# Cross-attention and quantized feed-forward on one core: the values are weighed between the two pairs of scores

## What is computed

```python
h = layernorm(x)
q = h @ Wq
k, v = split(concat(ctx, h) @ Wkv)          # 77 + 1024 keys, 16 heads of 16
dots = q @ k.T * 16 ** -0.5                  # per head
dots = where(j > i + 77, -inf, dots)         # a query sees the context and the rows up to its own
x = x + softmax(dots) @ v @ Wout + bout
h = layernorm(x)
x = x + quant_linear(gelu(quant_linear(h, w_fc)), w_proj)   # 256 -> 1024 -> 256
```

## Time and profile before

| | |
|---|---|
| median of 3 runs | 704.45 us |
| lowest and highest | 699.52 and 713.93 us |
| the profiled execution | 706.0 us |
| its span | 704.3 us |
| mean granted PE clock | 0.908 |
| PE busy | 605.6 us (86%) |
| VectorE busy | 424.8 us (60%) |
| ScalarE busy | 422.4 us (60%) |
| GpSimd busy | 217.7 us (31%) |

### The profile page before, as it was taken

The page is one execution under the profiler, slowest core; times in us unless marked ns, Lnnn a source line. Parts: engine busy times, 40 slices in busy tenths (PEclk is TensorE's granted clock), DMA queues, the critical chain, the costliest instruction groups (busy, mean ns, idle before and its releaser), DMA issues.

```text
span 704.3 us, 11805 instructions
## 1 busy us (share of the span) xinstructions
PE 605.6 (86%) x4138; PEld 265.5 (38%) x4147; DVE 424.8 (60%) x925; ACT 422.4 (60%) x555; POOL 217.7 (31%) x312
## 2 busy tenths in 40 slices
PE   8478887999998897997988899999998997978833
PEld 4323443334453342333543144334542463335411
DVE  5504869668755685498364468484277295374554
ACT  3165565688646964875565576876676565645701
POOL 3225601441526221441344212441435212121100
PEclk9879898999999998999998699999997797689975
DMA  4998921340499623092696203093896021003102
GB/s 142 123 168 141 106 80 41 75 53 16 71 112 130 92 61 105 1 120 55 87 120 99 39 16 88 4 112 62 106 136 84 16 61 46 16 16 62 31 15 46
DMA packets 77703, 52.04 MB, mean 74 GB/s; under 512 B 37771, under 2 KB 77319, under 8 KB 77626
## 3 DMA queue, kind: packets, MB, share of 16 engines
q1 hardware_dynamic: 77626, 51.02, 47.2%
HBM read 12.12 MB, written 4.19 MB: 23 GB/s over the span
## 4 chain that ended last, share of the span: by engine, by line
PE 52%; DVE 26%; issue 8%; DMA 6%; ACT 5%; SPq 2%; POOL 1%; DVEq 0%; ACTq 0%
PE psO L1222 15%; PE psS L1237 12%; PE psD L1157 6%; PE psD L1103 5%; DVE hid L870 4%; PE psD L1137 4%; PE psD L1155 3%; ACT probs L720 3%; DMA k_stack<-k_parts 3%; DVE amax L859 3%; PE psD L1166 3%; PE psD L1113 3%; DMA hT<-hq 2%; DVE hq L871 2%; DVE o_cols L990 2%
## 5 line engine op out<-in xcount | busy, mean ns | idle before, releaser
L720 ACT ACTIVATE probs<-psS 128x1024 f32<-128x1024 f32 (+4 forms) x392 | 329.5, 887 | 202.6 <-PE psS L1237 201.6
L663 POOL TENSOR_SCALAR_AFFINE_SELECT probs<-probs 128x512 f32<-128x512 f32 (+2 forms) x164 | 105.7, 656 | 375.9 <-ACT probs L720 375.9
L1237 PE MATMUL psS<-q_stack,k_stack 99*128 99x512 bf16 (+5 forms) x1008 | 201.8, 316 | 18.7 <-ACT probs L720 9.8
L1222 PE MATMUL psO<-probs,v_aug 128*17 128x512 f32 (+5 forms) x2016 | 184.5, 473 | 20.6 <-DVE o_cols L990 17.0
L1237 PEld LDWEIGHTS psS<-q_stack,k_stack 99*128 99x128 bf16 (+1 forms) x1008 | 81.2, 104 | 149.4 <-ACT probs L720 76.7
L1222 PEld LDWEIGHTS psO<-probs,v_aug 128*17 128x17 f32 (+1 forms) x2016 | 44.7, 99 | 110.0 <-issue 96.2
L859 DVE TENSOR_REDUCE amax<-hid 128x32 f32<-128x1024 f32 (+1 forms) x45 | 53.4, 1187 | 28.5 <-ACT hid L793 27.1
L990 DVE STREAM_TRANSPOSE o_cols<-psO 128x512 f32<-128x512 f32 (+1 forms) x36 | 23.5, 653 | 70.3 <-PE psO L1222 70.0
L870 DVE TENSOR_TENSOR hid<-hid,magic 128x1024 f32<-128x1024 f32 (+1 forms) x45 | 56.7, 1261 | 11.0 <-DMA hT<-hq 5.4
L793 ACT ACTIVATE hid<-psD 128x512 f32<-128x512 f32 x64 | 37.4, 597 | 43.0 <-PE psD L1157 42.6
L871 DVE TENSOR_TENSOR hq<-hid,magic 128x1024 bf16<-128x1024 f32 (+1 forms) x41 | 53.2, 1298 | 1.4
(11 more groups left out here) (90 smaller groups left out, 531.3 us busy)
## 6 DMA issues: line engine op xcount, KB each, us to landing
q_stack<-q_parts SPq DMA_DIRECT2D x96, 128.0 KB, 5.2
k_stack<-k_parts SPq DMA_DIRECT2D x48, 147.2 KB, 8.1
k_stack<-k_parts SPq DMA_DIRECT2D x48, 128.0 KB, 6.0
x_in<-in_x_dram SPq DMA_DIRECT2D x8, 512.0 KB, 4.6
x<-in_x_dram SPq DMA_DIRECT2D x8, 512.0 KB, 4.7
out_dram<-x SPq DMA_DIRECT2D x16, 256.0 KB, 2.2
hid<-in_L_ffn_w_fc_dram SPq DMA_DIRECT2D x1, 1024.0 KB, 17.1
hid<-in_L_ffn_w_proj_dram SPq DMA_DIRECT2D x1, 1024.0 KB, 5.0
```

What stands on the lines that cost most here:

```text
L663: last = pool.affine_select(out=tile, in_=tile, compare_op=ALU.is_ge, fill=0.0, base=first - (P * t - CTX), pattern=[[0, GH], [1, m]], cha ...
L720: act.activation(probs[:, k % PB, 2 * pair:2 * pair + 2, 0:n], psS[:, 2 * pair:2 * pair + 2, 0:n], ACT.Exp, scale=DH ** -0.5).then_inc(pro ...
L1222: last = pe.matmul(psO[SQ * j:SQ * j + VW, first - st.q0:first - st.q0 + n], v_aug[0:rows, v_tile(st.b, st.c, t), GH * st.g + j, :], probs ...
L1237: last = pe.matmul(psS[0:rows, j, off:off + n], k_stack[0:ROWS, GH * st.g + j, P * t:P * t + rows], q_heads(0, ROWS, st)[:, j, first - CHU ...
```

## The change

In each turn PE weighs the values after the first half's items and ahead of the second pair of scores, where it weighed them behind that pair. Nothing else is edited; the places in the table stay.

```diff
                 if 0 <= k < TOTAL:
                     for item in PLAN[k, 0]:
                         handle(item)
-                if k + 1 < TOTAL:
-                    score_pair(k + 1, 1)
                 if 1 <= k:
                     for n in PV_AT[k]:
                         pv(n)
+                if k + 1 < TOTAL:
+                    score_pair(k + 1, 1)
                 for item in PLAN[k, 1]:
                     handle(item)
```

## The result

The change makes the kernel slower: 726.23 us (median of 5 runs, 716.03 to 727.25) against 710.63 (5 runs), a ratio of 1.033 with a 95% interval of 1.020 to 1.045. Timed again beside other kernels it was 715.28 us (4 runs) against 708.59, 1.016 (1.004 to 1.028). The ratios leave out runs in a second, slower state that some executions fall into, so they are not the quotients of the medians, which are 1.022 and 1.009. The forecast was 708 us, within 697 to 719, and +3.7 us; the medians are +15.6 and +6.7 us apart.

What follows compares the result with a forecast made beforehand. PE, busy 86% of the span, was taken as the bound. Terms 3.4 + 1.7 + 2.4 + 2 - 1.8 - 2 - 2 = +3.7 us, on a median of 704.45, gave 708 us, range 697 to 719.

Steps and rivals of the forecast that it cites:

- Worth at most those 9.8 us: PE's waits for exponentials: giving PE work between two pairs of scores could by itself gain at most 9.8 us.
- the copy places: 15 places where ScalarE's copy falls behind the second exponential: PE waits 6.8 us in all, half taken, 3.4 us lost.
- Turns without items: 85 of 195 turns: the new order is the same cycle turned by one place, so the cost is nothing.
- The credit for score waits: Scores where two weighings now come ahead of the second pair: early waits go, -2 us, between 0 and -9.8.
- fc behind a second pair: Five fc runs: a later exponential delays the first gelu, so the fourth fc waits 0.35 us each, 1.7 us lost.
- The wait for psO and the masks: Second pair now behind four psO waits, 2.4 us lost; weighings come earlier behind later masks, 2 us lost.
- What comes earlier: A block's last weighing ends 0.44 us sooner: wout's waits for attT give -1.8 us, xqT's input -2.0 us.
- The signs: If right: score waits 13 to 20 us, on first pairs; attT below 7.5; psO near 17; ScalarE's score waits about 200.
- the slower rival: ScalarE's queue can't follow back-to-back exponentials in turns with items, PE waits: 721 us, +16.5 us; chance 0.13.
- The faster rival: VectorE's chain starts 0.44 us sooner at 14 places and weighings cover score waits: 693 us, 11 us gained; chance 0.14.
- Rival C: Posed with the experiments: whole kernel's time follows the granted clock, which got lower; no chance given.

Runs made afterwards that it cites:

- experiments 1: Against the kernel before, the weighing moved ahead of the second pair only in the 83 turns with first-half items: 723.17 us, 1.020.
- 7: Kernel before, with every exponential over half of its columns only: 710.37 us, 1.003 of the untouched kernel before.
- 8: Full change, with every exponential over half of its columns only: 702.29 us, 0.999 of the untouched kernel before.
- 9: Kernel before, but turns weighing two steps without first-half items put both weighings ahead of the second pair: 712.54 us, 1.012.
- 10: Kernel before, but turns weighing two steps put one weighing ahead of the second pair, the other behind: 711.74 us, no ratio.
- 11: Kernel before, with ScalarE's copies of first-half items ahead of its second exponential: 708.08 us, 1.003.
- number 2: Against the kernel before, the weighing moved ahead of the second pair only in the 112 turns without first-half items: 712.71 us, 1.006.
- 3: Full change, with ScalarE's copies of first-half items ahead of its second exponential: 717.46 us, 1.011 of before.
- 4: Full change, with all items of a turn in its second half: 712.46 us, 1.005 of before.
- 6: Full change, but the weighing stays behind the second pair in the 36 turns after a block's opening step: 716.74 us, 1.018 of before.

## Why the prediction was wrong

*The bound and the views.* Right: PE is the engine that sets the time, and its busy time didn't change. "Worth at most those 9.8 us" was right for a gain; it said nothing on how fast the same number can grow, and I took a small number of waits for room.

*Turns with items: the copy places.* The mechanism and the places were right, and the term was mis-sized in one move. Worked out were 6.8 us at 15 places; measured are 7.1 - 0.7 = 6.4 us. "I take half the sum, 3.4, as PE waits for VectorE or attT between most of them" is what failed: at most 2 of the 6.4 us can have been given back, as PE's waits for attT, xqT's input and psO fell by 5.8 us together, where 3.8 were forecast for other reasons. At the weighing of psO, the largest such wait, 16.3 us of 17.0 remain. That VectorE is fed by PE, so that the wait behind such a place starts later with it, would explain this; no run tests it. The Trainium skill (PSUM — Partial Sum Buffer, Engine vs sequencer instructions) says that ScalarE's queue is strictly first in, first out. The trace agrees with that order (cast at 133.88, exponential behind it at 134.34), and the undiscounted 6.8 us was the better guide.

*Turns without items.* "As a cycle these are the same string" is the step that failed outright. It holds only while each turn weighs once. The second turn of each block weighs nothing, and there the weighing of the turn before used to part the pairs. The third steps of the blocks carry about 18 us of excess instead of 7.7. Two of the copy places lie there and make 1.2 us of this; some 9 us remain, in a term that I had at nothing. Of the 12.3 us more on scores the copy places leave 5.9, which is these 9 us less the gain told next, with some small entries of both signs. That a turn weighs nothing stood in my own account of the kernel; the sum never used it.

*The credit for score waits,* -2 us, did come, and more: the second pairs of the blocks' fourth steps, ahead of which two weighings now stand, went from 3.6 us of excess to none, and the first pairs of these steps didn't take it over (3.9 to 3.5). The first pairs of later steps grew by 4.2 us; three copy places make half of that.

*fc behind a second pair.* 1.7 us forecast; the excess of the fc items rose by 1.6. Right.

*The wait for psO and the masks.* 2.4 and 2 us forecast. The masks came out near that, from 0.2 to 1.8 us of waits. The waits for psO stayed in four places, at 16.3 us. There the prediction didn't hold together: if PE comes a pair sooner and the wait's end stays, the waits themselves grow by the 2.4 us, and yet they were to stay near 17. They did, and the term was 0. The excess of all weighings rose by 1.7 us, so the two terms together were too high by 2.7.

*What comes earlier.* wout gained 3.7 us, twice the 1.8 forecast: the reason given covers 1.8, and what the rest comes from isn't shown (it may be what the copy places gave back). xqT gained 1.4 of 2.0.

*The sum* by the profiles is 6.4 + 5.9 + 1.6 + 1.7 - 3.7 - 1.4 = +10.5 us, where the two spans differ by 9.9; by the runs at equal clock it is +12 to +15. What lies between 10.5 and that is not accounted for. That 10.5 meets 9.9 is luck: steps 100 to 114 take 13 us less after the change, for a reason that none of the terms has (see the last section), and the rest of the span grew by 22.9 us in this profile, half of it where it has a stall that the second profile of the full change hasn't got. In that one the rest grew by 11.1 us, and this, as near as one profile tells it, is what the sum should be held against.

*The signs.* The score waits passed the 13 to 20 us that were to show the forecast right, without reaching the 25 of the slower rival, and moved to the first pairs. The waits for attT and psO did as was said. ScalarE's waiting for scores rose to 219 us instead of staying near 200.

*The rivals.* The slower rival, 721 us by ScalarE's queue, was nearest in size and in cause, with a chance of 0.13. It had the waits in the item turns, and experiments 1, 7 and 8 bear it out; its price per bare turn, 0.16 us in 68 places, isn't what the traces show (some 40 places besides those of the copies, with 0.2 to 0.6 us more each). The faster rival had its parts: VectorE's waits for psO fell by 15.6 us. But only about 5 us of that reached PE, and the cover, for which the Trainium skill (Perfetto Trace Analysis, Matmuls) advises to rotate groups of matmuls through the banks, was given in one turn and taken in the next. Rival C is refuted as the cause of the loss (the full change is 12 to 15 us slower at equal clock) and right for the spread.

## What to carry to other kernels

Two engines in lockstep see the order of work as one string over the turns. Write the string out for the turns that differ (here the one that weighs nothing) before calling a rotation free, and count the longest row of producers without other work between. A hidden engine with little slack, here two exponentials of 0.92 us against 1.87 us of PE work per step, can double PE's waits for it when such rows appear. And do not discount a loss on the engine that sets the time because a wait follows, unless what ends that wait is independent of this engine. A small change of order can also move something that isn't in the plan at all, as the stall of the next section; look for it before a sum that meets the span is taken for right.

## What the runs showed of the hardware

**The spread goes with the granted clock.** 0.01 of mean clock goes with 5.7 us of 708, in a kernel whose PE idles a seventh of the time. Part of it comes in single events. In the profile of before PE stands 3.39 us in the middle of a weighing, for which the view names no semaphore, and the clock falls behind it; these are windows before, around and behind it, in that profile and in the second one of the full change, which has no such event:

```profile
340.00:366.00 26.00, 25.86 (x183) 13.78 (x182) 12.47 (x37) 15.86 (x23) 8.68 (x15) 1.00 1.02 113
366.00:376.00 10.00, 6.61 (x45) 3.08 (x43) 4.06 (x8) 4.80 (x6) 3.92 (x6) 0.72 1.14 159
376.00:402.00 26.00, 21.98 (x113) 6.83 (x116) 14.61 (x24) 14.71 (x23) 9.61 (x13) 0.76 0.35 49
```

```profile
366.00:376.00 10.00, 9.85 (x76) 4.84 (x76) 7.43 (x27) 6.78 (x10) 2.40 (x5) 1.00 1.16 121
376.00:402.00 26.00, 22.14 (x166) 8.36 (x164) 16.36 (x30) 18.98 (x28) 14.81 (x21) 1.00 0.80 115
```

**The stall stands at one place of the program, and the change takes it away there.** It is the weighing of step 102, ahead of its last two matmuls:

```profile
366.64 0.88 PE L1222 MATMUL psO<-probs,v_aug 128*17 128x333 f32 x14
370.92 0.41 PE L1222 MATMUL psO<-probs,v_aug 77*17 77x77 f32 x2 [3.39 <-issue]
```

The profiles of before and of experiments 1, 7, 9, 10 and 11 have it there, with 2.64 to 4.34 us, and that of number 2 right behind this weighing, with 3.11 us. None of the six profiles of the full change and of the kernels made from it (3, 4, 6 and 8) has one at this step; in the first profile of the full change the same weighing is

```profile
378.64 0.89 PE L1222 MATMUL psO<-probs,v_aug 128*17 128x333 f32 x16
```

From the weighing of step 100 to that of step 114 before takes 53.0 us and the full change 40.0 in both of its profiles, by the stall and by the lower clock behind it. So the change gives back 13 us here, and costs more elsewhere than the spans tell. The first profile of the full change has its own stall, 4.47 us within step 151's weighing, and takes 41.6 us from there to step 160 where the second takes 30.0; that their spans read 714.2 and 702.4 us, with equal waits of PE, is this. A change of 1 to 2% can't be read from two spans.

What PE stands for isn't shown. In the seven profiles with the stall at step 102 a packet of 16 KB of the page's instruction queue q8 (1.7 us on the way in before) starts 0.3 to 1.9 us behind the start of this weighing; in the six without it one starts 3.1 to 4.9 us ahead of it (and in number 4 another 2.2 us behind). That points to the loading of the program, and no run here tests it.

**Changing between weighings and scores costs PE 0.2 us for the way there and back,** 0.09 into the weighing of four heads side by side and 0.11 out of it, as told at experiment 10.
